# Gate and up by Strassen's scheme in a four-layer residual kernel: seven block products for eight

## The chip, the cores and the metric

The kernel runs on one core of one Trainium2 chip. The metric is the device time of one execution in microseconds (us); lower is better. Three executions of the kernel before took 313.84, 312.49 and 316.62 us, median 313.84.

## The reference, cut to what matters

`x` is 8 batches of 128 tokens with 512 features, all float32. Four layers follow one another, and each adds its result to `x`. Layers 0 to 2 (a weight matrix chosen by each batch's id; a routed low-rank layer; a low-rank layer with a bias) stay as they are. The change is in layer 3, a gated MLP of 1376 hidden features, padded to 11 chunks of 128, with rank-16 additions chosen by batch:

```
def lora_add(base, inp, A, B):
    Ab = A[layer_idx][lora_indices]
    Bb = B[layer_idx][lora_indices]
    t = jnp.einsum('bri,bni->bnr', Ab, inp)
    return base + jnp.einsum('bor,bnr->bno', Bb, t) * SCALE
gate = lora_add(jnp.einsum('bnh,fh->bnf', x, W_gate), x, A_gate, B_gate)
up = lora_add(jnp.einsum('bnh,fh->bnf', x, W_up), x, A_up, B_up)
act = jax.nn.silu(gate) * up
down = lora_add(jnp.einsum('bnf,hf->bnh', act, W_down), act, A_down, B_down)
```

## The kernel before

Everything lies with features on the 128 partitions and the 1024 tokens (two halves `h` of 512) along the free dimension. PE (TensorE) multiplies in fp32r. To keep float32 accuracy each operand is split into a high part, the fp32r copy made by ACT (`high`, line 436), and a low part, the difference made by DVE (`low`, line 619). One product of weights 128x128 with 512 tokens is then three matmuls, lines 967 to 969 (`split_product`).

Gate and up of one chunk `fc` take, for each half and for each of gate and up (`g`), four feature blocks by three matmuls, 12 in all (`gate_up_main`), and then two matmuls of 256 columns that add the ranks (`gate_up_lora`, line 1076, on `bgu_st` and `t3_st`). The sum gathers in one PSUM bank (banks 4 to 7). When the gate bank is done ACT takes its silu into `act_f` (line 558); when the up bank is done DVE multiplies (`act_product`, line 829). Each engine has its own in-order program and they meet at semaphores. Ten of the eleven chunks run in loops of two chunks on every engine. While PE works on a chunk, ACT and DVE split the next chunk's weights (`gate_up_hi`, `gate_up_lo`), and SP loads the chunk after that: one transfer `wgu` and eight transfers `bgu`, one for each batch (`load_gate_up`, lines 357 and 360).

Ahead of the loops stands the entry to layer 3: `thin3` (1052) and `sum_ranks` (1063) make the ranks of `x`, which ACT and DVE write to `t3_st` (436 and 820), and PE does chunk 0 between them. After the loops come the ranks of the down layer (`down_ranks`, line 1123, 176 small matmuls), and then the down product, 22 pieces of at least 12 matmuls, whose activations ACT and DVE split into a ring of eight buffers. In this kernel `wd` is split during the last two chunks of gate and up.

## Time and profile before

| what | us |
|---|---|
| median of three executions | 313.84 |
| the profiled execution | 312.77 |
| its span, first to last instruction | 310.8 |
| PE busy | 302.0 (97%) |
| DVE busy | 146.8 (47%) |
| ACT busy | 106.8 (34%) |

The span leaves about 2 us of the profiled execution's time outside. The busy share of an engine is an average over stages. A PE row's duration overlaps the next one's: the step from one row's start to the next one's is what a matmul costs, and it is read from the timeline.

### The profile page before, as it was taken

How to read it: one execution, taken by the hardware profiler on the slowest of the kernel's cores; microseconds unless marked ns; L12 is line 12 of the kernel's file. 1: busy time of each engine (PE TensorE's matmuls, PEld its weight loads, DVE VectorE, ACT ScalarE, POOL GpSimd, SP SyncE). 2: the span in 40 equal slices, each digit the busy share in tenths (PEclk: the TensorE clock that was granted, in tenths of full speed). 3: DMA queues.
4: the chain of work that ended last, by engine and by line, in shares of the span. 5: the costliest groups of instructions: out<-in, count | busy, mean ns of one | idle time of the engine just before them, and what ended most of it. 6: DMA issues, size and time to landing. Idle time of an engine off the chain costs nothing.

```text
span 310.8 us, 4638 instructions
## 1 busy us (share of the span) xinstructions
PE 302.0 (97%) x1690; PEld 249.1 (80%) x1690; DVE 146.8 (47%) x253; ACT 106.8 (34%) x169; POOL 11.2 (4%) x25
## 2 busy tenths in 40 slices
PE   6799999999999999999999999999999999999995
PEld 5357878988888888888888888888888888888884
DVE  1298898977559336144044043142624833233003
ACT  2377762504335245124034033133532641221000
POOL 1020000800100000000000000000000000000000
PEclk9999999999999999999999999999999999999999
DMA  5989990005206500431421421460520000022004
GB/s 170 343 306 350 396 307 24 2 27 183 63 10 179 160 19 1 137 102 33 135 95 40 135 85 50 146 268 0 162 67 0 2 2 0 0 70 68 0 2 135
DMA packets 23888, 33.21 MB, mean 107 GB/s; under 512 B 3264, under 2 KB 16064, under 8 KB 23744
## 3 DMA queue, kind: packets, MB, share of 16 engines
q1 hardware_dynamic: 23584, 32.48, 32.1%
q10 hardware_dynamic: 288, 0.52, 0.6%
q8 instruction: 10, 0.16, 0.2%
q14 instruction: 6, 0.05, 0.0%
HBM read 30.89 MB, written 2.10 MB: 106 GB/s over the span
## 4 chain that ended last, share of the span: by engine, by line
PE 91%; DMA 3%; SPq 2%; DVE 2%; ACT 1%; issue 0%
PE bank L967 25%; PE bank L968 25%; PE bank L969 25%; PE bank L1076 3%; DMA w_raw<-in_w 3%; PE bank L921 3%; PE bank L1123 2%; PE bank L951 1%; PE bank L1014 1%; PE bank L901 1%; PE bank L953 1%; PE bank L952 1%; PE bank L943 1%; SPq L310 1%; PE bank L1052 1%; PE bank L1023 1%
## 5 line engine op out<-in xcount | busy, mean ns | idle before, releaser
L967 PE MATMUL bank<-xb,wgu_hl 128*128 128x512 f32 x176 | 69.3, 394 | 0.0
L968 PE MATMUL bank<-xb,wgu_hl 128*128 128x512 f32 x176 | 69.0, 392 | 0.0
L969 PE MATMUL bank<-xb,wgu_hl 128*128 128x512 f32 x176 | 68.5, 389 | 0.0
L829 DVE TENSOR_TENSOR act_f<-bank,act_f 128x512 f32 (+1 forms) x22 | 15.2, 692 | 79.4 <-PE bank L1076 75.0
L969 PEld LDWEIGHTS bank<-xb,wgu_hl 128*128 128x128 f32 x176 | 33.1, 188 | 7.2
L967 PEld LDWEIGHTS bank<-xb,wgu_hl 128*128 128x128 f32 x176 | 33.0, 188 | 5.9 <-issue 0.2
L968 PEld LDWEIGHTS bank<-xb,wgu_hl 128*128 128x128 f32 x176 | 33.2, 189 | 5.2
L967 PE MATMUL bank<-act_hl,wd_hl 128*128 128x512 f32 (+1 forms) x99 | 36.5, 369 | 0.0
L968 PE MATMUL bank<-act_hl,wd_hl 128*128 128x512 f32 (+1 forms) x99 | 36.3, 367 | 0.0
L969 PE MATMUL bank<-act_hl,wd_hl 128*128 128x512 f32 (+1 forms) x99 | 36.2, 366 | 0.0
L558 ACT ACTIVATE act_f<-bank 128x512 f32 (+1 forms) x22 | 13.2, 598 | 64.6 <-PE bank L1076 64.6
L619 DVE TENSOR_TENSOR w_hl<-w_raw,w_hl 128x512 fp32r<-128x512 f32 x29 | 19.2, 693 | 9.7 <-ACT w_hl L436 9.7
L619 DVE TENSOR_TENSOR act_hl<-act_f,act_hl 128x512 fp32r<-128x512 f32 x22 | 14.4, 689 | 18.9 <-ACT act_hl L436 18.8
L436 ACT ACTIVATE w_hl<-w_raw 128x512 fp32r<-128x512 f32 x29 | 17.7, 625 | 12.4 <-DMA w_raw<-in_w 12.3
L436 ACT ACTIVATE act_hl<-act_f 128x512 fp32r<-128x512 f32 x22 | 12.9, 626 | 25.3 <-PE bank L969 22.0
L969 PEld LDWEIGHTS bank<-act_hl,wd_hl 128*128 128x128 f32 x99 | 18.6, 188 | 3.1
L967 PEld LDWEIGHTS bank<-act_hl,wd_hl 128*128 128x128 f32 x99 | 18.7, 189 | 3.0 <-issue 0.2
L968 PEld LDWEIGHTS bank<-act_hl,wd_hl 128*128 128x128 f32 x99 | 18.7, 189 | 2.7
L1076 PEld LDWEIGHTS bank<-t_st,bgu_st 128*128 128x128 f32 x88 | 16.1, 188 | 3.5 <-DVE t_st L820 0.2
L436 ACT ACTIVATE wgu_hl<-wgu_raw 128x1024 fp32r<-128x1024 f32 x11 | 11.7, 1061 | 18.4 <-PE bank L1076 18.4
L1076 PE MATMUL bank<-t_st,bgu_st 128*128 128x256 f32 x88 | 17.2, 282 | 0.0
L436 ACT ACTIVATE xb<-x_f 128x512 fp32r<-128x512 f32 x16 | 10.0, 628 | 16.9 <-DVE x_f L739 12.8
(124 smaller groups left out, 418.0 us busy)
## 6 DMA issues: line engine op xcount, KB each, us to landing
w_raw<-in_w SPq DMA_DIRECT2D x22, 256.0 KB, 8.0
wgu_raw<-in_wgu SPq DMA_DIRECT2D x11, 512.0 KB, 3.4
bgu_raw<-in_bgu SPq DMA_DIRECT2D x88, 64.0 KB, 2.2
w_raw<-in_w SPq DMA_DIRECT2D x7, 512.0 KB, 7.8
wd_raw<-in_wd SPq DMA_DIRECT2D x4, 704.0 KB, 5.3
out<-x_f SPq DMA_DIRECT2D x7, 256.0 KB, 2.3
...
```

Source lines behind the costliest of these rows:

```text
L310: _, ids = nc.values_load_multi_w_load_instructions(src[0:1, 0:B], engines=[mybir.EngineType.SP], min_val=0, max_val=last, skip_runtime_bo ...
L436: return act.activation(dst, src, ACT.Copy)
L558: act.activation(act_f[:, fc, h * HT:(h + 1) * HT], bank[4 + 2 * h][:], ACT.Silu).then_inc(silu_done, 1)
L619: return dve.tensor_tensor(dst, src, hi.bitcast(F32), ALU.subtract)
L829: dve.tensor_tensor(dst, bank[5 + 2 * h][:], dst, ALU.mult).then_inc(act_mul, 1)
L901: ins = pe.transpose(dst[:, k * P:(k + 1) * P], src, ident[:])
L921: ins = pe.matmul(thin1_bank(h, j)[:, 0:2 * TM1], xb[:, k, c, cols], aw1_hl[:, c].rearrange("p k n -> p (k n)"), start=(c == 0 and k == 0) ...
L967: pe.matmul(dst, w_hi, x[0][:, cols], start=start, stop=False)
L968: pe.matmul(dst, w_hi, x[1][:, cols], start=False, stop=False)
L969: return pe.matmul(dst, w_lo, x[0][:, cols], start=False, stop=stop)
L1076: ins = pe.matmul(bank[4 + 2 * h + g][:, q * 2 * S:(q + 1) * 2 * S], bgu_st[slot][:, pair, g], t3_st[:, g, pair * 2 * S:(pair + 1) * 2 * S ...
L1123: ins = pe.matmul(bank[h][32 * j:32 * j + R, 0:S], ad_raw[:, b, fc], act_f[:, fc, b * S:(b + 1) * S], start=(fc == 0), stop=(fc == FC - 1))
```

## The change

Chunk 0 stays. The other ten chunks are taken in five pairs, and for each pair gate and up apart, so ten steps `n` (even: gate, odd: up). In one step the 256 output features, 512 input features and 1024 tokens are cut in two each way. The eight block products become seven, in Winograd's form of Strassen's scheme: DVE forms four sums of weight blocks in each step (`form_s`, 128x256 each) and, once, four sums of blocks of `x` (`form_t`, 128x1024 each), all of which are split into high and low as well. Products share banks: ACT copies four partial results of each step from PSUM to SBUF (`copy_part`), and DVE adds them to the finished banks (`add_c`). Silu and the multiplication then read SBUF. Each step has the same eight rank matmuls per two chunks that it had before.

The rank weights of two chunks come in one transfer per batch (`load_bgu`), into one buffer. The loops are written out. The splitting of `wd` moves behind gate and up, piece by piece with the activations. The selection matrices are loaded and spread somewhat later.

The core of the diff:

```diff
...
+            def load_wgu(fc):
+                sp.dma_start(wgu_raw[raw_slot(fc)][:], wgu[fc]).then_inc(wgu_in[raw_slot(fc)], 16)
+            def load_bgu(p):
+                f1, f2 = chunks_of(2 * p)
                 for b in range(B):
                     rows = slice(64 * (b % 2), 64 * (b % 2) + 64)
-                    sp.dma_start(bgu_raw[slot][rows, b // 2], bgu[adapter3[b], fc]).then_inc(bgu_in[slot], 16)
+                    sp.dma_start(bgu_raw[rows, :, b // 2],
+                                 bgu[adapter3[b], f1:f2 + 1].rearrange("f r n -> r f n")).then_inc(bgu_in, 16)
...
-            with sp.Fori(0, 4) as i:
-                for u in range(2):
-                    fc = 2 * i + 2 + u
-                    sp.wait_ge(wgu_lo, 2 * i + 1 + u)
-                    sp.wait_ge(bgu_ready, 2 * i + 1 + u)
-                    load_gate_up(fc, u)
-            sp.wait_ge(wgu_lo, FC - 2)
-            sp.wait_ge(bgu_ready, FC - 2)
-            load_gate_up(FC - 1, 0)
-            sp.wait_ge(bgu_ready, FC)
+            sp.wait_ge(wgu_lo, 1)
+            sp.wait_ge(bgu_ready, 1)
+            sp.wait_ge(main_done, 16)
+            load_bgu(0)
+            load_wgu(3)
+            load_wgu(4)
+            for p in range(1, PAIRS):
+                sp.wait_ge(bgu_ready, bgu_count(2 * p - 1, 1))
+                load_bgu(p)
+                if p + 1 < PAIRS:
+                    sp.wait_ge(wc_lo, 3 * 2 * p)
+                    load_wgu(2 * p + 3)
+                    load_wgu(2 * p + 4)
+            sp.wait_ge(bgu_ready, bgu_count(2 * PAIRS - 1, 1))
+            sp.wait_ge(wc_lo, 3 * 2 * PAIRS)
+            for o in range(C):
+                sp.dma_start(wd_raw[:, o], wd[o]).then_inc(wd_in[o], 16)
...
+            def copy_part(n, k):
+                done, b = ((p1_done, 0), (p5_done, 2), (p6_done, 0), (p7_done, 0))[k]
+                act.wait_ge(done, n + 1)
+                if n == 0:
+                    act.wait_ge(xt_lo, 2)
+                if n >= 2:
+                    act.wait_ge(silu_done if n % 2 == 0 else act_mul, H + 4 * (n // 2))
+                high(part[n % 2][k][:], bank[4 * (n % 2) + b][:]).then_inc(part_copied, 1)
+            def silu(p, k):
+                i, h = c_place(k)
+                fc = chunks_of(2 * p)[i]
+                act.wait_ge(c_added, 8 * p + k + 1)
+                act.activation(act_f[:, fc, h * HT:(h + 1) * HT], part[0][C_PART[k]][:], ACT.Silu).then_inc(silu_done, 1)
...
+                if g == 1:
+                    for k in (2, 3):
+                        silu(p, k)
+                if more:
+                    wc_high(n + 1, 0)
+                copy_part(n, 0)
+                copy_part(n, 1)
+                if more:
+                    wc_high(n + 1, 1)
+                copy_part(n, 2)
+                if more:
+                    wc_high(n + 1, 2)
+                if g == 0:
+                    for k in (0, 1):
+                        silu(p, k)
+                copy_part(n, 3)
+                if more:
+                    for i in range(2):
+                        bgu_high(n + 1, i)
...
+            act.wait_ge(c22_ready, 2 * PAIRS)
+            for i in range(5):
+                wd_high(i)
+                if i == 0:
+                    act.wait_ge(act_mul, 2 * FC)
                 act_high(i)
...
+            def form_s(n, k):
...
+                    ins = dve.tensor_tensor(s_tmp[:, 0], a["21"], a["22"], ALU.add)
+                elif k == 1:
+                    dve.wait_ge(s_formed, 4 * n + 1)
+                    ins = dve.tensor_tensor(s_tmp[:, 1], s_tmp[:, 0], a["11"], ALU.subtract)
+                elif k == 2:
+                    ins = dve.tensor_tensor(s_tmp[:, 2], a["11"], a["21"], ALU.subtract)
+                else:
+                    dve.wait_ge(s_formed, 4 * n + 3)
+                    ins = dve.tensor_tensor(s_tmp[:, 3], a["12"], s_tmp[:, 1], ALU.subtract)
+                ins.then_inc(s_formed, 1)
...
+            def form_t(k):
+                b11, b12, b21, b22 = (x_f[:, h * HB:(h + 1) * HB, 2 * d:2 * d + 2] for d in range(2) for h in range(H))
+                if k == 0:
+                    dve.wait_ge(x_sum, number(2, 1, 1) + 1)
+                    ins = dve.tensor_tensor(tx[0][:], b12, b11, ALU.subtract)
+                elif k == 1:
+                    dve.wait_ge(x_sum, number(2, 1, 3) + 1)
+                    dve.wait_ge(xt_formed, 1)
+                    ins = dve.tensor_tensor(tx[1][:], b22, tx[0][:], ALU.subtract)
+                elif k == 2:
+                    ins = dve.tensor_tensor(tx[2][:], b22, b12, ALU.subtract)
+                else:
+                    dve.wait_ge(xt_formed, 2)
+                    ins = dve.tensor_tensor(tx[3][:], b21, tx[1][:], ALU.subtract)
+                ins.then_inc(xt_formed, 1)
...
             residual(2, 0, [])
             t2_uv_low(1)
-            gate_up_lo(0, 0, 1)
+            odd_lo()
             t2_low(1)
-            gate_up_lo(1, 1, 2)
-            residual(2, 1, [])
+            for k in (0, 2, 1, 3):
+                form_s(0, k)
+            for part_of in range(3):
+                wc_low(0, part_of)
+            x_add(2, 1, 0)
+            x_add(2, 1, 1)
+            x_low(2, 1, 0)
+            form_t(0)
+            x_low(2, 1, 1)
+            x_add(2, 1, 2)
+            x_low(2, 1, 2)
+            x_add(2, 1, 3)
+            form_t(1)
+            x_low(2, 1, 3)
+            for k in range(2, 4):
+                form_t(k)
...
+            def add_c(n, k):
+                ready, b = ((c11_ready, 1), (c12_ready, 2), (c21_ready, 3), (c22_ready, 0))[k]
+                dve.wait_ge(ready, n + 1)
+                dve.wait_ge(part_copied, 4 * n + C_PART[k] + 1)
+                dst = part[n % 2][C_PART[k]]
+                dve.tensor_tensor(dst[:], bank[4 * (n % 2) + b][:], dst[:], ALU.add).then_inc(c_added, 1)
+            def act_product(p, k):
+                i, h = c_place(k)
+                dst = act_f[:, chunks_of(2 * p)[i], h * HT:(h + 1) * HT]
+                dve.wait_ge(silu_done, H + 4 * p + k + 1)
+                dve.wait_ge(c_added, 8 * p + 4 + k + 1)
+                dve.tensor_tensor(dst, part[1][C_PART[k]][:], dst, ALU.mult).then_inc(act_mul, 1)
...
-            act_product(0, 0)
+            for k in range(3):
+                xt_low(k)
+            odd_product(0)
+            for k in (0, 2, 1, 3):
+                form_s(1, k)
             t3_low(1)
+            odd_product(1)
+            for i in range(2):
+                bgu_low(0, i)
+            xt_low(3)
+            for n in range(2 * PAIRS):
+                p, g = divmod(n, 2)
+                more = n + 1 < 2 * PAIRS
+                if more and n > 0:
+                    form_s(n + 1, 0)
+                    form_s(n + 1, 2)
+                if n > 0:
+                    for k in (2, 3):
+                        add_c(n - 1, k)
+                if more:
+                    if n > 0:
+                        form_s(n + 1, 1)
+                    wc_low(n + 1, 0)
+                    if n > 0:
+                        form_s(n + 1, 3)
+                if n > 0 and g == 0:
+                    for k in (2, 3):
+                        act_product(p - 1, k)
+                add_c(n, 0)
+                if g == 1:
+                    act_product(p, 0)
+                if more:
+                    for part_of in (1, 2):
+                        wc_low(n + 1, part_of)
+                add_c(n, 1)
+                if g == 1:
+                    act_product(p, 1)
+                if more:
+                    for i in range(2):
+                        bgu_low(n + 1, i)
             for h in range(H):
                 zero_td_bank(h)
...
+            for k in (2, 3):
+                add_c(2 * PAIRS - 1, k)
+                act_product(PAIRS - 1, k)
...
+            def product(dst, n, a, x, start, stop):
+                w = wc[1 - n % 2]
+                for c in range(2):
+                    hi, lo = w[:, 0, a, c], w[:, 1, a, c]
+                    pe.matmul(dst[:], hi, x[0][c], start=(start and c == 0), stop=False, skip_group_check=True)
+                    pe.matmul(dst[:], hi, x[1][c], start=False, stop=False, skip_group_check=True)
+                    ins = pe.matmul(dst[:], lo, x[0][c], start=False, stop=(stop and c == 1), skip_group_check=True)
+                return ins
+            def step3(n):
+                p, g = divmod(n, 2)
+                f1, f2 = chunks_of(n)
+                x, w, y, z = (bank[4 * g + k] for k in range(4))
+                pe.wait_ge(wc_lo, 3 * n + 1)
+                if n >= 2:
+                    pe.wait_ge(c_added, 4 * (n - 1))
+                product(x, n, A11, x_block(0, 0), True, True).then_inc(p1_done, 1)
+                product(w, n, A12, x_block(1, 0), True, False)
+                pe.wait_ge(bgu_ready, bgu_count(n, 0))
+                lora3(w, f1, g, 0).then_inc(c11_ready, 1)
+                pe.wait_ge(wc_lo, 3 * n + 2)
+                if n == 0:
+                    pe.wait_ge(xt_lo, 1)
+                product(y, n, S1, t_block(0), True, True).then_inc(p5_done, 1)
+                pe.wait_ge(part_copied, 4 * n + 1)
+                if n == 0:
+                    pe.wait_ge(xt_lo, 2)
+                product(x, n, S2, t_block(1), False, True).then_inc(p6_done, 1)
+                pe.wait_ge(part_copied, 4 * n + 2)
+                product(y, n, S4, x_block(1, 1), False, False)
+                lora3(y, f1, g, 1).then_inc(c12_ready, 1)
+                pe.wait_ge(part_copied, 4 * n + 3)
+                if n == 0:
+                    pe.wait_ge(xt_lo, 3)
+                product(x, n, S3, t_block(2), False, True).then_inc(p7_done, 1)
+                pe.wait_ge(wc_lo, 3 * n + 3)
+                if n == 0:
+                    pe.wait_ge(xt_lo, 4)
+                product(z, n, A22, x_block(0, 1), True, False)
+                pe.wait_ge(bgu_ready, bgu_count(n, 1))
+                lora3(z, f2, g, 0).then_inc(c21_ready, 1)
+                pe.wait_ge(part_copied, 4 * n + 4)
+                lora3(x, f2, g, 1).then_inc(c22_ready, 1)
...
```

The places that the prediction speaks of, in each engine's own order. First ACT, one odd step before: here the loop over one chunk, between two silu.

```order
L436 ACTIVATE wgu_hl_89<-wgu_raw_85 128x1024 [waits up_done]
L436 ACTIVATE bgu_st_87<-bgu_raw_83 128x1024 [waits bgu_in1]
L557 ISA
L558 ISA [waits gate_done]
L558 ACTIVATE act_f<-bank 128x512
```

And ACT now, in the whole of step 3 (odd; `wc_gate` holds the weights of step 4, `part_0` and `part_1` are the partial results of gate and of up, whose last digits number buffers).

```order
L664 ACTIVATE act_f<-part_3_101 128x512 [waits c_added]
L664 ACTIVATE act_f<-part_1_99 128x512 [waits c_added]
L498 ACTIVATE wc_gate<-wgu_raw_88 128x512 [waits wgu_in3,wgu_in2,c21_ready]
L498 ACTIVATE part_0_102<-bank 128x512 [waits act_mul,p1_done]
L498 ACTIVATE part_1_103<-bank 128x512 [waits act_mul,p5_done]
L498 ACTIVATE wc_gate<-s_tmp 128x1024 [waits s_formed]
L498 ACTIVATE part_2_104<-bank 128x512 [waits act_mul,p6_done]
L498 ACTIVATE wc_gate<-wgu_raw_89 128x256
L498 ACTIVATE part_3_105<-bank 128x512 [waits act_mul,p7_done]
L498 ACTIVATE bgu_st_84<-bgu_raw 128x4x128 [waits c22_ready,bgu_in]
L498 ACTIVATE bgu_st_83<-bgu_raw 128x4x128 [waits c22_ready,bgu_in]
```

Two silu and a weight split now stand ahead of the first copy of a partial result.

DVE ahead of them, from the end of step 2 into step 3.

```order
L924 SCALAR_TENSOR_TENSOR bgu_st_84<-bgu_st_84,lo_rows_128,bgu_raw 128x4x128 [waits bgu_hi]
L924 SCALAR_TENSOR_TENSOR bgu_st_83<-bgu_st_83,lo_rows_128,bgu_raw 128x4x128 [waits bgu_hi]
L946 TENSOR_TENSOR s_tmp<-wgu_raw_89 128x256 [waits wc_lo,wgu_in3,wgu_in2]
L951 TENSOR_TENSOR s_tmp<-wgu_raw_88,wgu_raw_89 128x256
L1038 TENSOR_TENSOR part_3_101<-bank,part_3_101 128x512 [waits part_copied,c21_ready]
L1038 TENSOR_TENSOR part_1_99<-bank,part_1_99 128x512 [waits part_copied,c22_ready]
```

The two sums that the silu need stand behind two splits of rank weights and two weight sums. Before, nothing of this was on DVE.

DVE at the entry to layer 3, between the end of `t2` and the first rank write `t_st` (before: two `x_f` at once, no `tx`).

```order
L869 SCALAR_TENSOR_TENSOR x_f<-bank,bias_sb,x_f 128x4x128 [waits main_done]
L749 TENSOR_TENSOR xb<-x_f,xb 128x512 [waits x_hi]
L869 SCALAR_TENSOR_TENSOR x_f<-bank,bias_sb,x_f 128x4x128 [waits main_done]
L976 TENSOR_TENSOR tx_94<-x_f,tx_93 128x1024 [waits xt_formed,x_sum]
L749 TENSOR_TENSOR xb<-x_f,xb 128x512 [waits x_hi]
L978 TENSOR_TENSOR tx_95<-x_f 128x1024
L981 TENSOR_TENSOR tx_96<-x_f,tx_94 128x1024 [waits xt_formed]
L1022 SCALAR_TENSOR_TENSOR t_st<-t_st,hi_lo,bank 64x2x128 [waits t3_hi,hi_lo_copied]
```

The three `tx` rows (`form_t`) now stand ahead of the rank write.

## Rows read from the trace of the kernel before

**Rows 1.** The page: busy us, share of the span, instructions.
```profile
PE 302.0 (97%) x1690; PEld 249.1 (80%) x1690; DVE 146.8 (47%) x253; ACT 106.8 (34%) x169; POOL 11.2 (4%) x25
```
**Rows 2.** The page: chain that ended last, share of the span by engine.
```profile
PE 91%; DMA 3%; SPq 2%; DVE 2%; ACT 1%; issue 0%
```
**Rows 3.** Stretches: us, busy PE, PEld, DVE, ACT, POOL; granted clock, DMA share, GB/s.
```profile
0.00:42.60 42.60, 37.29 (x164) 26.16 (x165) 27.47 (x51) 25.05 (x45) 3.11 (x9) 1.00 0.91 318
...
103.40:119.60 16.20, 16.20 (x138) 13.47 (x138) 6.88 (x14) 6.17 (x14) 0.00 (x0) 1.00 0.23 70
119.60:238.80 119.20, 119.20 (x565) 99.44 (x567) 41.75 (x42) 35.33 (x43) 0.00 (x0) 1.00 0.29 95
```
**Rows 4.** Timeline in one chunk: start us, us, engine, line, operation, [idle before].
```profile
179.05 0.40 PE L967 MATMUL bank<-xb,wgu_hl 128*128 128x512 f32 x1
...
181.80 0.40 PE L1076 MATMUL bank<-t_st,bgu_st 128*128 128x256 f32 x2
182.03 0.40 PE L967 MATMUL bank<-xb,wgu_hl 128*128 128x512 f32 x1
...
182.32 0.60 ACT L558 ACTIVATE act_f<-bank 128x512 f32 x1 [1.06 <-PE bank L1076]
...
183.60 5.05 SPq L360 DMA_DIRECT2D bgu_raw<-in_bgu  x8
...
185.01 0.40 PE L967 MATMUL bank<-xb,wgu_hl 128*128 128x512 f32 x1
...
185.39 0.69 DVE L829 TENSOR_TENSOR act_f<-bank,act_f 128x512 f32 x1 [2.62 <-PE bank L1076]
```
**Rows 5.** Groups by line and form: count, busy us, mean ns, idle before.
```profile
L619 DVE TENSOR_TENSOR act_hl<-act_f,act_hl 128x512 fp32r<-128x512 f32 x22 | 14.4, 689 | 18.9 <-ACT act_hl L436 18.8
L797 DVE SCALAR_TENSOR_TENSOR bgu_st<-bgu_st,lo_rows,bgu_raw 128x1024 fp32r<-128x1024 f32 x11 | 14.1, 1278 | 0.0
L619 DVE TENSOR_TENSOR wgu_hl<-wgu_raw,wgu_hl 128x1024 fp32r<-128x1024 f32 x11 | 13.5, 1225 | 2.4 <-ACT wgu_hl L436 2.4
L436 ACT ACTIVATE act_hl<-act_f 128x512 fp32r<-128x512 f32 x22 | 12.9, 626 | 25.3 <-PE bank L969 22.0 <-DVE act_f L829 3.2
L436 ACT ACTIVATE wgu_hl<-wgu_raw 128x1024 fp32r<-128x1024 f32 x11 | 11.7, 1061 | 18.4 <-PE bank L1076 18.4
L829 DVE TENSOR_TENSOR act_f<-bank,act_f 128x512 f32 x16 | 11.1, 692 | 62.9 <-PE bank L1076 62.9
L558 ACT ACTIVATE act_f<-bank 128x512 f32 x16 | 9.6, 600 | 51.1 <-PE bank L1076 51.1
```
**Rows 6.** Timeline, ACT and DVE: six instructions in a row without a gap.
```profile
239.71 3.23 ACT L436 ACTIVATE act_hl<-act_f 128x512 fp32r<-128x512 f32 x6 [3.24 <-DVE act_f L829]
240.37 3.70 DVE L619 TENSOR_TENSOR act_hl<-act_f,act_hl 128x512 fp32r<-128x512 f32 x6 [0.76 <-ACT act_hl L436]
```
**Rows 7.** The page: DMA issues, count, KB each, us from issue to landing.
```profile
bgu_raw<-in_bgu SPq DMA_DIRECT2D x88, 64.0 KB, 2.2
...
wd_raw<-in_wd SPq DMA_DIRECT2D x4, 704.0 KB, 5.3
```
**Rows 8.** Timeline of DVE and of PE at the entry to layer 3.
```profile
96.03 1.23 DVE L619 TENSOR_TENSOR wgu_hl<-wgu_raw,wgu_hl 128x1024 fp32r<-128x1024 f32 x1
98.37 1.40 DVE L739 SCALAR_TENSOR_TENSOR x_f<-bank,bias_sb,x_f 128x512 f32<-128x512 f32 x2
108.84 2.02 DVE L820 SCALAR_TENSOR_TENSOR t_st<-t_st,hi_lo,bank 64x256 fp32r<-64x256 f32 x4 [3.18 <-ACT t_st L436]
116.80 2.01 DVE L820 SCALAR_TENSOR_TENSOR t_st<-t_st,hi_lo,bank 64x256 fp32r<-64x256 f32 x4 [1.76 <-ACT t_st L436]
...
112.00 0.74 PE L1076 MATMUL bank<-t_st,bgu_st 128*128 128x256 f32 x4
118.93 0.69 PE L1076 MATMUL bank<-t_st,bgu_st 128*128 128x256 f32 x4
```
**Rows 9.** The chain in order of time: start us, us, what (the down ranks).
```profile
238.82 4.93 PE bank L1123 x176
```

349 lines of the change are left out of this document (210 added, 139 removed).

## The prediction, made before the changed kernel had run

> **What bounds the kernel now.** I read the busy shares first: PE is busy for 302.0 of 310.8 us, DVE for 47% and ACT for 34% [rows 1]. Then the chain: PE holds 91% of it [rows 2]. Then the stretches: in the loops over chunks 1 to 10, 119.60 to 238.80, PE is busy without a gap and its granted clock is 1.00, that is 2.4 GHz, while DVE works 41.75 and ACT 35.33 of 119.20 us [rows 3]. So removed PE work is worth its full time there, as long as DVE and ACT stay ahead. Last the timeline of one chunk, for prices. The twelve matmuls of 512 columns run from 179.05 to 181.80, 0.229 us each, and the two rank matmuls from 181.80 to 182.03, 0.23 us [rows 4]; a group repeats every 2.98 us (182.03 to 185.01). The 0.40 beside each row overlaps its neighbours and is no price.
>
> **PE.** Before, two chunks of gate (or up) took 2 x 2 x 12 = 48 matmuls of 512 columns and 8 of 256. A step now takes 7 products x 2 feature blocks x 3 = 42, and the same 8. Ten steps save 60 matmuls x 0.229 = **13.7 us**. A step lasts 42 x 0.229 + 4 x 0.23 = 10.55 us where it was 4 x 2.98 = 11.92. The form (128x128 weights, 512 columns) doesn't change. Within a step, counted from its start, P1 ends at 1.37, c11 is ready at 2.98, P5 ends at 4.35 and P6 at 5.72, c12 is ready at 7.3, P7 ends at 8.7, c21 is ready at 10.3, c22 at 10.55.
>
> **DVE and ACT in a step.** DVE takes 689 ns for 512 elements and 1225 for 1024 [rows 5], so about 1.05 ns an element, and by that line 0.42 us for 256. In a queue without waits six of 512 take 3.70 us, so 0.60 from one to the next, 0.09 less than one alone; on ACT six take 3.23, so 0.52, 0.10 less [rows 6]. The rank split (1278 for 1024 [rows 5]) gives 0.74 for 512. A DVE step: four weight sums 4 x 0.42, four `add_c` 4 x 0.69, three weight splits 0.69 + 1.23 + 0.42, two products 2 x 0.69, two rank splits 2 x 0.74 = 9.7 us alone, 8.4 when queued (15 instructions, 0.09 less each). That is 80 to 92% of 10.55, where it was 35% [rows 3]. ACT: splits 0.63 + 1.06 + 0.41, four copies and two silu at 0.60 [rows 5], two rank copies at 0.63 = 7.0 alone, 5.9 queued. Neither is the bound by its sum; what matters is the round trip through both.
>
> **The round trip.** PE to ACT takes 0.29 us (the group ends at 182.03, silu starts at 182.32), PE to DVE 0.38 (185.01 to 185.39) [rows 4]. P7 ends at 8.7, so its copy starts at 9.0 and the two rank copies at 9.5 and 10.0; DVE splits them at 10.2 and 10.8 and is free at 11.5, that is 0.9 into the next step. There come two weight sums (0.9, 1.25), then `add_c` for c21 and c22 (1.6 and 2.2, done at 2.9). In an **odd** step ACT's queue has silu of these two first: at 2.35 and 3.0, then the weight split at 3.5, then the copy of P1 at 4.0, done at 4.6. PE needs it at 4.35, to add P6 to the same bank. With 0.1 us to take the signal up, PE waits about 0.4 us. In an **even** step ACT has no silu there, and P1's copy starts at 1.7; later `silu(p, 1)` needs `add_c` of c12, at 7.75 to 8.45 on DVE, so P7's copy starts at 9.1 and is done at 9.7, where PE needs it at 10.3: no wait. The last odd step has no weight split, and no wait. So 4 x 0.4 = **+1.6 us**, between 0 (hand-overs 0.1 shorter at four places) and 4.8 (twelve instructions of the round trip each 0.07 longer).
>
> Here DVE reads PSUM in `add_c`. The product that reads a bank takes 692 ns, the split from SBUF 689 [rows 5], so the sum takes one price for both. The Trainium skill (VectorE: DVE Perf Modes, "The TRN2 errata") gives a PSUM source 62 cycles more on VectorE, 0.065 us; by it the two `add_c` on the round trip would add 0.13 us in each of four odd steps, +0.5. The two rows, equal but for 3 ns, don't show that.
>
> **The entry.** DVE starts a weight split at 96.03 and reaches `x_add` of the second half at 98.37 [rows 8]. Now four weight sums and three splits stand there, with ACT's splits between: sums to 97.6 (four steps, one link dependent), the second split can start when ACT's 1.06 us copy is done, at 98.8, and the last ends at 100.3. `x_add` comes 1.9 us later; PE took up that half's work well after it. But `form_t` adds four of 1.23 us, and DVE reaches the first rank write at about 110.9, done (2.02 us) at 112.9, where it was 108.84 to 110.86; PE wants the ranks at 112.00 [rows 8], so it waits 0.9. Behind it stand three splits of `xt` (3.4 queued), a product, four sums (1.6): the second rank write starts at 118.7 and ends at 120.7, where PE, 0.9 late, wants it at 119.8: another 0.9. Together **+1.8 us**; bounds 0.5 (if the queue spacing holds at each place) and 4 (if each of some twenty instructions takes 0.1 longer).
>
> **The end.** `wd` is no longer split beforehand. It is loaded after the last rank split, 1 us into step 9. One transfer of 704 KB of the four took 5.3 us in the median [rows 7]; four at once I take as at most 9.5, which ends at the end of the step. The last two `add_c` and products end 2.7 us after the step; then ACT 0.63 and DVE 0.69: the first piece is ready 4.3 us after it, and PE's down ranks cover 4.93 [rows 9]. Afterwards a piece costs DVE 1.2 and PE some 2.7. I take **+0.2**, bounds 0 and 2.5 (a load later by two). The later selection matrices and the POOL work lie on no chain: +0. One transfer per batch halves the issues (eight took 5.05 us on SP [rows 4]), which ran beside PE and are worth nothing.
>
> **Sum.** -13.7 + 1.6 + 1.8 + 0.2 = -10.1 us. Against the profiled execution (312.77) that gives 302.7; the median of the three stands 1.07 higher and gives 303.7. I take **303.2**.
>
> **Rivals.**
> - *The round trip is wider.* For it: DVE at up to 92%, and 25 instructions a step that wait for another engine. Against it: queued spacing is 0.09 shorter than durations. If each of twelve links costs 0.1 more, odd steps lose 1.2 more (x4) and even steps, with 0.6 of slack in P7's copy, 0.3 (x5): +6.3, about **309.5**. Chance 0.15.
> - *No wait at all.* The walk was pessimistic, or PE's own starts drift late enough to cover it: 313.3 - 13.7 = **299.6**. Chance 0.10.
> - *The one rank buffer makes it slower.* The new load starts only after the second rank split of the odd step, 1.2 us into it, its last issue goes out at 6.3 and lands at 8.5 if it takes the 2.2 us of the row [rows 7] though it is twice as large. ACT wants it at 9.5; PE itself only 3.0 us into the next step, at 13.5, so a landing after about 12.2 delays PE, in four steps. From 14.7 on (8.4 us from issue to landing) the 10.1 us are gone, and at 16.4 it is **320**. Against it: DMA is at 0.29 in that stretch [rows 3]. Chance 0.03.
> - *The clock falls.* PE now waits for ACT inside a step. Before, PE was idle for 5.3 of the first 42.6 us and the clock stayed at 1.00 [rows 3], so short waits did not lower it here. One step at 1.2 GHz would cost 10.5 us more: **313.7**. Chance 0.04. The Trainium skill (TensorE: Matmul & The Clock Gate, "A second HAM failure mode: psum-queue depth-cycling") tells of a kernel that cycled through PSUM banks, idled briefly between groups and had its clock switch back and forth; the loops here cycled through four banks at 1.00, which speaks against it.
>
> **How the numbers follow.** My forecast has 0.68, with 300.5 to 307 as its own spread from the bounds. The range 299.5 to 308.5 takes in that, half of the case without waits and a third of the wider round trip: about 0.78. Two per cent, which is about what can be told from no change here (the three executions differ by 1.3%), is 6.3 us: faster means below 307.6. Forecast, no wait and a fifth of the wider round trip: 0.81. Within 2%: the rest of it and the clock, 0.16. Slower: 0.03.
>
> **What the profile after would show.** PE with 60 matmuls fewer and steps of 10.55 us (even) and 10.9 (odd), 0.229 from start to start. A PE gap before the first matmul that adds P6 in odd steps, put down to ACT's copy, none in even steps. DVE at 8 to 9.7 busy us a step. PE gaps of about 0.9 before the two rank groups at the entry, put down to DVE's `t_st`. No gap after the down ranks. I'm wrong if even steps show gaps, if ACT waits for `bgu_raw`, if a wait at the end stands on `wd`, or if the clock is below 1.00.

## The result, and the profile of the changed kernel

The changed kernel takes **302.89 us** (median of four executions, 302.5 to 303.19) where the kernel before takes 313.74 (312.49 to 316.62): a ratio of 0.9642, with a 95% interval of 0.9605 to 0.9679. The forecast was 303.2. The profiled execution took 302.71 us, of which the span is 300.9; before, these were 312.77 and 310.8.

The page first: busy time, share of the span and instructions of each engine, and then the chain of work by engine.

```profile
PE 290.3 (96%) x1630; PEld 237.4 (79%) x1630; DVE 204.4 (68%) x378; ACT 142.4 (47%) x250; POOL 10.7 (4%) x25
PE 64%; DVE 13%; SPq 7%; DMA 6%; issue 4%; ACT 4%; DVEq 0%; ACTq 0%
```

60 matmuls are gone from PE. Against [rows 1] DVE has 57.6 us more work and ACT 35.6. PE's part of the chain falls from 91% [rows 2] to 64%, which looks like a new bound but isn't one: PE is still busy for 96% of the span. The chain now crosses places where PE waited for a few tenths, and from there it follows the engine that released it far back. Only the stretches tell how much such a place costs.

The stretches of both kernels, cut at the same events: the first rank matmul of layer 3, the first matmul of step 0, the first matmul of the down ranks. Columns as in [rows 3]. Before:

```profile
103.41:119.45 16.04, 16.04 (x137) 13.31 (x137) 6.88 (x14) 6.02 (x14) 0.00 (x0) 1.00 0.23 71
119.45:238.82 119.37, 119.37 (x566) 99.61 (x568) 41.75 (x42) 35.48 (x43) 0.00 (x0) 1.00 0.29 95
```

After, with one even step (step 0), one odd step (step 1) and the down ranks behind them:

```profile
103.74:121.38 17.64, 16.61 (x137) 13.24 (x137) 15.99 (x24) 9.39 (x18) 0.96 (x1) 1.00 0.37 120
121.38:228.74 107.36, 106.94 (x503) 88.06 (x501) 81.11 (x140) 62.58 (x109) 0.00 (x0) 1.00 0.28 96
121.38:132.00 10.62, 10.62 (x53) 8.86 (x52) 7.09 (x10) 8.65 (x15) 0.00 (x0) 1.00 0.00 0
132.00:142.81 10.81, 10.81 (x52) 8.74 (x51) 8.23 (x16) 6.00 (x11) 0.00 (x0) 1.00 0.51 161
228.74:233.66 4.92, 4.92 (x177) 4.71 (x176) 4.61 (x8) 2.76 (x6) 0.00 (x0) 1.00 0.46 132
```

The span is 9.9 us shorter. Ten steps give 119.37 - 107.36 = 12.01. The entry takes 1.60 of it back (16.04 to 17.64), and layer 3 starts 0.33 later (103.41 to 103.74), ahead of everything that the diff puts behind it. From the first down-rank matmul to the end it is 71.9 before and 72.2 after, 0.2 more; of this the down ranks are 4.85 and 4.92 (up to 243.67 and 233.66, the first matmuls of the down product). The granted clock is 1.00 in every stretch. DVE works 8.1 us in a step of 10.7, ACT 6.3.

The ten steps last 10.62, 10.81, 10.61, 10.82, 10.60, **11.25**, 10.61, 10.81, 10.61 and 10.62 us. So four odd steps are longer, and one of them more than the others.

The entry, on PE: the three rows before which PE waited, in the same view as [rows 8].

```profile
107.94 1.16 PE L1308 MATMUL bank<-t_sb,t_sel 128*128 128x128 f32 x8 [0.17 <-ACT t_sb L498]
...
113.26 0.71 PE L1321 MATMUL bank<-t_st,bgu_st 128*128 128x256 f32 x4 [0.40 <-DVE t_st L1022]
...
120.81 0.74 PE L1321 MATMUL bank<-t_st,bgu_st 128*128 128x256 f32 x4 [0.46 <-DVE t_st L1022]
```

And DVE there:

```profile
100.46 1.40 DVE L869 SCALAR_TENSOR_TENSOR x_f<-bank,bias_sb,x_f 128x512 f32<-128x512 f32 x2
...
111.10 2.01 DVE L1022 SCALAR_TENSOR_TENSOR t_st<-t_st,hi_lo,bank 64x256 fp32r<-64x256 f32 x4
...
118.74 2.01 DVE L1022 SCALAR_TENSOR_TENSOR t_st<-t_st,hi_lo,bank 64x256 fp32r<-64x256 f32 x4
```

The two rank writes start at 111.10 and 118.74, and PE takes each up 0.15 and 0.06 us after its end. DVE is late by its queue, without idle time in front of either row.

The round trip of step 5, the long one, which starts at 174.84. DVE's sum is done, ACT runs two silu, then a weight split, then the copy of P1, and PE takes up P6:

```profile
177.49 1.23 ACT L664 ACTIVATE act_f<-part 128x512 f32<-128x512 f32 x2 [2.23 <-DVE part L1038]
...
179.77 0.50 PE L1342 MATMUL bank<-xt,wc_up 128*128 128x512 f32 x1 [0.42 <-ACT part L498]
```

In steps 1, 3 and 7 the same place shows no bracket, and has to be read from the starts. This is step 1, which starts at 132.00:

```profile
134.21 1.23 ACT L664 ACTIVATE act_f<-part 128x512 f32<-128x512 f32 x2 [2.23 <-DVE part L1038]
135.35 0.61 ACT L498 ACTIVATE wc_gate<-wgu_raw 128x512 fp32r<-128x512 f32 x1
135.87 1.28 ACT L498 ACTIVATE part<-bank 128x512 f32<-128x512 f32 x2
...
136.13 0.39 PE L1344 MATMUL bank<-xt,wc_up 128*128 128x512 f32 x1
136.50 0.50 PE L1342 MATMUL bank<-xt,wc_up 128*128 128x512 f32 x1
136.84 0.39 PE L1343 MATMUL bank<-xt,wc_up 128*128 128x512 f32 x1
```

From start to start these take 0.37 and 0.34 us where the neighbours take 0.23: 0.25 more in all. The first is the matmul that adds P6 into P1's bank, and the copy ahead of it began at 135.87.

Two readings were not forecast. The load of rank weights, on SP's queue and on ACT, which waits for it in steps 1 and 3 (they start at 132.00 and 153.42):

```profile
133.08 6.14 SPq L413 DMA_DIRECT2D bgu_raw<-in_bgu  x8
...
142.11 1.15 ACT L498 ACTIVATE bgu_st<-bgu_raw 128x512 fp32r<-128x512 f32 x2 [0.33 <-DMA bgu_raw<-in_bgu]
...
154.50 6.08 SPq L413 DMA_DIRECT2D bgu_raw<-in_bgu  x8
...
163.96 1.15 ACT L498 ACTIVATE bgu_st<-bgu_raw 128x512 fp32r<-128x512 f32 x2 [0.76 <-DMA bgu_raw<-in_bgu]
```

Eight issues take 6.1 us, 0.77 each, where eight of half the size took 5.05 [rows 4]. They land 3.5 and 4.0 us after the last of them started (138.62 and 159.97, see the last section), and so 10.1 and 10.5 us into the step. The page has 2.7 for the median where it had 2.2 [rows 7]:

```profile
bgu_raw<-in_bgu SPq DMA_DIRECT2D x40, 128.0 KB, 2.7
```

Last the end. ACT splits the first piece of the activations 2.8 us after the steps' end, and DVE's part of it is done at 232.88, 0.78 ahead of PE, which leaves the down ranks at 233.66:

```profile
231.53 0.63 ACT L498 ACTIVATE act_hl<-act_f 128x512 fp32r<-128x512 f32 x1 [2.06 <-DVE act_f L1045]
...
232.19 0.69 DVE L749 TENSOR_TENSOR act_hl<-act_f,act_hl 128x512 fp32r<-128x512 f32 x1
```

### The profile page after: what moved, and what is told of

Its sections match the earlier page's. It is cut to its first block, busy times and chain, and to the rows that moved or that the text cites. A ratio compares the mean times of both kernels' runs of the same rounds, so it can differ in the third digit from the quotient of the medians.

```text
span 300.9 us, 4565 instructions
## 1 busy us (share of the span) xinstructions
PE 290.3 (96%) x1630; PEld 237.4 (79%) x1630; DVE 204.4 (68%) x378; ACT 142.4 (47%) x250; POOL 10.7 (4%) x25
## 4 chain that ended last, share of the span: by engine, by line
PE 64%; DVE 13%; SPq 7%; DMA 6%; issue 4%; ACT 4%; DVEq 0%; ACTq 0%
PE bank L1212 11%; PE bank L1213 11%; PE bank L1214 11%; PE bank L1342 6%; PE bank L1343 6%; PE bank L1344 6%; DMA w_raw<-in_w 4%; SPq L413 3%; SPq L358 3%; DMA bgu_raw<-in_bgu 2%; PE bank L1321 2%; PE bank L1166 2%; DVE bgu_st L924 2%; DVE part L1038 2%; PE bank L1416 2%
## 5 line engine op out<-in xcount | busy, mean ns | idle before, releaser
L498 ACT ACTIVATE part<-bank 128x512 f32<-128x512 f32 x40 | 23.7, 595 | 26.8 <-PE bank L1344 26.2
L1038 DVE TENSOR_TENSOR part<-bank,part 128x512 f32<-128x512 f32 x40 | 26.7, 685 | 5.1 <-PE bank L1321 3.8
L924 DVE SCALAR_TENSOR_TENSOR bgu_st<-bgu_st,lo_rows,bgu_raw 128x512 fp32r<-128x512 f32 (+1 forms) x21 | 15.4, 773 | 14.3 <-ACT bgu_st L498 14.3
L498 ACT ACTIVATE act_hl<-act_f 128x512 fp32r<-128x512 f32 x22 | 13.6, 624 | 20.8 <-PE bank L1214 18.8
L664 ACT ACTIVATE act_f<-part 128x512 f32<-128x512 f32 x20 | 12.5, 632 | 15.7 <-DVE part L1038 15.7
L1072 DVE TENSOR_TENSOR x_f<-bank,x_f 128x512 f32<-128x512 f32 (+1 forms) x9 | 5.5, 629 | 19.5 <-PE bank L1437 19.5
L1321 PEld LDWEIGHTS bank<-t_st,bgu_st 128*128 128x128 f32 x88 | 14.7, 188 | 3.9 <-DVE t_st L1022 0.9
L1321 PE MATMUL bank<-t_st,bgu_st 128*128 128x256 f32 x88 | 15.8, 284 | 0.9 <-DVE t_st L1022 0.9
L1344 PE MATMUL bank<-xb,wc_gate 128*128 128x512 f32 x40 | 15.7, 394 | 0.0
L1343 PE MATMUL bank<-xb,wc_gate 128*128 128x512 f32 x40 | 15.7, 392 | 0.0
L1342 PE MATMUL bank<-xb,wc_up 128*128 128x512 f32 x40 | 15.6, 391 | 0.0
L1343 PE MATMUL bank<-xb,wc_up 128*128 128x512 f32 x40 | 15.6, 390 | 0.0
```

What stands on the lines that cost most here:

```text
L498: return act.activation(dst, src, ACT.Copy)
L664: act.activation(act_f[:, fc, h * HT:(h + 1) * HT], part[0][C_PART[k]][:], ACT.Silu).then_inc(silu_done, 1)
L924: return dve.scalar_tensor_tensor(out=st, in0=st.bitcast(F32), scalar=lo_rows16[:, 0:1], in1=raw, op0=ALU.mult, op1=ALU.add)
L1038: dve.tensor_tensor(dst[:], bank[4 * (n % 2) + b][:], dst[:], ALU.add).then_inc(c_added, 1)
L1321: ins = pe.matmul(dst[:, q * 2 * S:(q + 1) * 2 * S], bgu_st[fc % 2][:, pair, g], t3_st[:, g, pair * 2 * S:(pair + 1) * 2 * S], start=False ...
L1342: pe.matmul(dst[:], hi, x[0][c], start=(start and c == 0), stop=False, skip_group_check=True)
```

## Experiments

**Theory.** PE's work is the gain. It is short by a wait for P1's copy in four odd steps, set by the length of the round trip (DVE's sums, ACT's silu, ACT's split, ACT's copy) and not by how much DVE or ACT do in a step. **Rivals:** DVE, at 8.1 us a step, is near its bound, so that any work added to it costs time; the combining frame of the scheme costs PE something of its own; and the merged load of rank weights, which I had called worthless, carries part of the result. Step lengths are given throughout, since the profiled executions reach layer 3 anywhere between 102.9 and 104.7 us, while the ten steps of the two kernels that were profiled twice agree within 0.2%. Each kernel was timed beside the kernel before on the same chip (313.46, 313.59, 313.25 and 313.17 us in the four groups).

### The changed kernel again, and the two waits taken away one by one

The first group has the changed kernel itself, as it stands.

> The changed kernel once more, unedited, so that the three edits of this group are compared with it on the same chip. 302.9 us, 10.9 below the kernel before; odd steps of 10.8 us, the third of them (step 5) up to 0.4 longer, even steps of 10.6 us.

Measured: 303.25 us, ratio 0.9689 (0.9663 to 0.9714). Entry 17.65, steps 107.56 together, step 5 again the longest (11.39).

Then P1's copy, ahead of the silu in odd steps:

```diff
                 if g == 1:
+                    copy_part(n, 0)
                     for k in (2, 3):
                         silu(p, k)
                 if more:
                     wc_high(n + 1, 0)
-                copy_part(n, 0)
+                if g == 0:
+                    copy_part(n, 0)
                 copy_part(n, 1)
```

> Edit: in odd steps ACT copies the first partial result (P1) ahead of the two silu and the weight split, not behind them. Theory (the round trip through DVE and ACT makes PE wait for that copy in odd steps): the wait goes and every step takes 10.62 us; the trace of the changed kernel has the four odd steps 0.20, 0.20, 0.63 and 0.20 us above that, so 1.2 us less than the unedited kernel, 301.7. Rival (the extra length of odd steps is bank switching or a weight load, not the copy): no change, 302.9, with the gap still ahead of the first S2 matmul.

Measured: 301.64 us, ratio 0.9640 (0.9613 to 0.9667); entry 17.65, steps 105.76 together: 10.61, **10.53**, 10.60, **10.54**, 10.60, **10.53**, 10.60, **10.53**, 10.60, 10.62. ACT in step 1, which starts at 132.13 here:

```profile
133.71 0.60 ACT L498 ACTIVATE part<-bank 128x512 f32<-128x512 f32 x1 [1.60 <-PE bank L1346]
134.35 1.23 ACT L664 ACTIVATE act_f<-part 128x512 f32<-128x512 f32 x2
```

The copy is done at 134.31, and PE gets to P6 some 4.35 us into the step, at 136.5, and the wait is gone in all four steps. An odd step without it takes 10.53, less than an even one. So the round trip costs 0.28 us in steps 1, 3 and 7, which is about what the starts above show, and 0.72 in step 5: 1.56 together, and that is all that steps 0 to 9 lose to waits.

Next the entry: `form_t(3)` behind the first rank write, the second rank write ahead of the product and the weight sums, and ACT's split of `xt` out of the way.

```diff
-            for k in range(2, 4):
-                form_t(k)
+            form_t(2)
...
             t3_low(0)
+            form_t(3)
             for k in range(3):
                 xt_low(k)
+            t3_low(1)
             odd_product(0)
             for k in (0, 2, 1, 3):
                 form_s(1, k)
-            t3_low(1)
             odd_product(1)
```

> Edit: at the entry to layer 3 the rank writes t_st come earlier in DVE's and ACT's queues: the fourth sum of x blocks behind the first rank write, the first product of chunk 0 and the weight sums of step 1 behind the second, and on ACT the copy of the second sum of x blocks behind the first rank copy. Theory (PE waits there for DVE's queue alone): the gaps of 0.40 and 0.46 us before the two groups of rank matmuls go, with the slower restart after each, and step 0 begins 1.1 us earlier: 301.8. Rival (what is moved comes back as a wait in steps 0 and 1, where xt, the rank split and the product of chunk 0 are then late): 302.9, with new gaps in step 0.

Measured: 301.31 us, ratio 0.9628 (0.9605 to 0.9650). The entry takes 16.50 and step 0 10.82, 0.21 more than before the edit, since its first rank matmul now waits for DVE's split of `bgu_st`. Step 5 takes 10.80: its extra 0.44 is gone, although nothing in it was edited. In this execution ACT waited for the load of rank weights by 0.08 us in step 1 and not at all in step 3, where it had waited 0.76; the experiments on the load, below, return to this.

> Both edits, of ACT's order in odd steps and of the entry. If the two waits are separate, the gains add: 2.3 us less than the unedited kernel, 300.6. If one hides the other, 301.7.

Measured: 301.06 us, ratio 0.9611 (0.9587 to 0.9636). By stage both gains are there (entry 16.52, steps 105.97: 2.5 us less than the changed kernel; step 5's extra 0.44, which either edit alone also lost, counts once). The median is only 0.25 us under that of the entry edit alone and lies between the two forecasts; the profiled execution reached layer 3 at 104.65, about 1 us later than the others. In a second group, below, the median is 300.65.

### Is the removed work worth its full time?

The eighth product comes back, in the place where a step has its last one. The kernel counts A22 twice in c21; everything else of the scheme stays.

```diff
                 product(z, n, A22, x_block(0, 1), True, False)
+                product(z, n, A22, x_block(0, 1), False, False)
                 pe.wait_ge(bgu_ready, bgu_count(n, 1))
```

> Edit: an eighth product in each of the ten steps: the product of A22 is made twice into its bank, behind P7 (its rows of gate and up come out too large by it). It gives back the 60 matmuls. Theory (the gain is removed PE work and nothing else, and the odd steps' wait is a round trip from P7 to the next step, which now has 1.36 us more): 60 x 0.227 = +13.6 us, less the 1.2 us of waits, +12.4: 315.3, so 1 to 2 us slower than the kernel before, with all steps at 12.0. Rival (sharing banks and writing the loops out are worth something by themselves): 313.7 or less. Rival (the waits stay): 316.5.

Measured: 315.66 us, ratio 1.0068 (1.0041 to 1.0095), without a PE wait in a step.

```profile
121.16:240.55 119.39, 119.39 (x563) 99.59 (x561) 81.74 (x140) 62.27 (x109) 0.00 (x0) 1.00 0.26 86
```

With 48 matmuls of 512 columns a step the ten steps take 119.39 us, and 119.37 in the kernel before. So 40 us of new DVE work and 27 of new ACT work (41.75 to 81.74, 35.48 to 62.27) cost PE nothing while it ran, and what the scheme costs outside PE's count is the 2.07 us by which this kernel is slower: the entry (17.64, 1.6 more) and 0.5 elsewhere. Against the 105.76 of the kernel with P1's copy first, 60 matmuls make 13.6 us, 0.227 each. With a longer step the wait in odd steps vanished too, as a round trip from P7 asks: the eighth product stands behind P7, so ACT and DVE have 1.4 us more until the next step.

### The trip, or the load on DVE?

One instruction of 0.68 us more on DVE in each of four odd steps (it sums `x_f` into a scratch tile). In the first kernel, whose edit is shown, it stands on the trip, ahead of the sums of c21 and c22; in the second it stands later in the same step, ahead of the first rank split, where DVE was idle.

```diff
+        scratch = own("scratch", [2 * PAIRS, C])
...
                     form_s(n + 1, 2)
+                if more and g == 1:
+                    dve.tensor_reduce(scratch[:, n], x_f[:, 0], AX_X, ALU.add)
```

> Edit: one more DVE instruction (a sum over 512 elements of x into a scratch tile, about 0.6 us) in steps 1, 3, 5 and 7, between the weight sums and the two add_c, that is on the round trip from P7 to the copy of P1. Theory (the wait is the round trip): each of the four steps grows by about 0.6 us, +2.4: 305.3, and the wait before the first S2 matmul is 0.8. Rival (DVE's sum counts, not its place): same as the other placing of it.

> Edit: the same DVE instruction in the same four steps, but ahead of the first rank split, where DVE waits 1 to 1.9 us for ACT. Theory: +0, 302.9, though DVE is as busy as with the other placing. Rival (DVE's sum counts): +2.4, 305.3.

Measured: on the trip 305.37 us, ratio 0.9744 (0.9714 to 0.9774); in the gap 303.12, ratio 0.9666 (0.9642 to 0.9691). Steps 110.02 and 107.68 together. DVE and PE in step 1 of the kernel with it on the trip (one more line stands above, so 1038 is 1039 here):

```profile
133.59 0.68 DVE L1094 TENSOR_REDUCE scratch<-x_f 128x4 f32<-128x512 f32 x1
134.18 1.28 DVE L1039 TENSOR_TENSOR part<-bank,part 128x512 f32<-128x512 f32 x2
...
137.18 0.50 PE L1345 MATMUL bank<-xt,wc_up 128*128 128x512 f32 x1 [0.55 <-ACT part L499]
```

The same instruction costs 2.34 us in the one place and nothing in the other. PE waits 0.55 before P6; by the starts, P6's second matmul comes 0.83 later than in a step without a wait, where 0.8 was forecast. DVE has slack; the path has none. The even steps of both kernels are 0.16 us longer, which is not the instruction's doing; see the last section.

### The load of rank weights

The load as it was, one transfer per batch and chunk, but into the one raw buffer (ACT waits for each half by its own semaphore):

```diff
-                f1, f2 = chunks_of(2 * p)
-                for b in range(B):
-                    rows = slice(64 * (b % 2), 64 * (b % 2) + 64)
-                    sp.dma_start(bgu_raw[rows, :, b // 2],
-                                 bgu[adapter3[b], f1:f2 + 1].rearrange("f r n -> r f n")).then_inc(bgu_in, 16)
+                for i, fc in enumerate(chunks_of(2 * p)):
+                    for b in range(B):
+                        rows = slice(64 * (b % 2), 64 * (b % 2) + 64)
+                        sp.dma_start(bgu_raw[rows, i, b // 2],
+                                     bgu[adapter3[b], fc]).then_inc((bgu_in, bgu_in2)[i], 16)
```

> Edit: the rank weights of a pair come in two transfers per batch again, 16 issues in place of 8, all else as in the changed kernel. My prediction held the merging to be worth nothing. Theory now, by the trace of the changed kernel (8 issues took 6.1 us, landing came 3.5 to 4.0 us after the last, 10.1 to 10.5 us into the odd step, and ACT already waited up to 0.8 us for it): 16 issues at 0.63 take 10 us and land 14 us after the start of the odd step, 3.4 us into the even one; ACT's queue is then blocked ahead of the copy of P1, and PE waits 1 to 2 us in each of four even steps and somewhat in the odd step behind: +4 to +9 us, 307 to 312. Rival (hidden anyway): 302.9.

Measured: 313.05 us, ratio 0.9977 (0.9956 to 0.9998), 1 us above the forecast range. The steps take 116.80 us together, 9.4 more. In steps 1 and 2, which start at 132.07 and 142.90:

```profile
133.16 10.93 SPq L413 DMA_DIRECT2D bgu_raw<-in_bgu  x16
...
145.70 0.63 ACT L498 ACTIVATE bgu_st<-bgu_raw 128x512 fp32r<-128x512 f32 x1 [3.31 <-DMA bgu_raw<-in_bgu]
...
146.76 1.32 ACT L498 ACTIVATE part<-bank 128x512 f32<-128x512 f32 x2
...
150.29 1.06 ACT L498 ACTIVATE wc_up<-s_tmp 128x1024 fp32r<-128x1024 f32 x1 [2.21 <-DVE s_tmp L954]
151.25 0.58 ACT L498 ACTIVATE part<-bank 128x512 f32<-128x512 f32 x1
...
151.88 0.50 PE L1342 MATMUL bank<-xt,wc_gate 128*128 128x512 f32 x1 [1.24 <-ACT part L498]
```

Sixteen issues hold SP for 10.93 us, and the load lands 13.6 us after the start of step 1. ACT stands in its queue in front of the load, 3.31 us, and with it stand the weight splits and the copies of step 2 that are queued behind. The copy of P1, where the wait was forecast, is only 0.12 late for PE in step 2. The large wait stands 9 us into step 2, at the copy of P6: DVE's rank split is late by ACT's, its weight sums stand behind it, ACT's split of these sums waits for them (2.21), and P6's copy stands behind that split. Nowhere does PE wait for the rank weights themselves. So with one raw buffer nearly all of the kernel's gain hangs on the halved count of issues. Sixteen issues with a raw buffer for each chunk, as the kernel before had them, were not run in the changed kernel; whether they would have stayed hidden is open.

Then the other end: no load at all after the first pair. Every step uses the first pair's rank weights.

```diff
-                load_bgu(p)
...
-                act.wait_ge(bgu_in, 16 * B * (n // 2 + 2))
+                act.wait_ge(bgu_in, 16 * B * 2)
```

> Edit: the rank weights are loaded for the first pair only and used for all five (the ranks of the other four pairs come out wrong by it); nothing waits for those transfers. Theory (the extra 0.4 us of step 5 began as ACT's wait for bgu_raw in step 3): ACT has no wait on bgu_raw, all four odd steps are 10.8, total -0.4: 302.5. Rival (step 5's extra wait has another origin): step 5 still 11.25.

Measured: 302.12 us, ratio 0.9644 (0.9606 to 0.9682). Steps 10.58, 10.83, 10.60, 10.81, 10.61, **10.82**, 10.60, 10.81, 10.61, 10.62. The 0.28 in the odd steps stays, and step 5 is one of four equals. The place that waited 0.42 in the changed kernel:

```profile
178.78 0.50 PE L1341 MATMUL bank<-xt,wc_up 128*128 128x512 f32 x1
```

So the 0.44 that step 5 loses beyond the others comes from the load. The other kernels say the same by degrees. ACT's wait for the load is followed two steps later by a longer odd step: 0.76 by 0.44 in the changed kernel, 0.92 by 0.57 and 0.39 by 0.06 when it ran again. Waits of 0.33 (the changed kernel, step 1) and 0.24 (the added instruction in the gap, step 3) are followed by nothing. By these five, some 0.33 us of the wait is free and the rest is passed on one for one. The way from the load to step 5, by rows of the changed kernel, is this: ACT's wait of 0.76 in step 3 puts the rank splits late, so that DVE sums c12 of step 4 late, and silu waits for it, and P7's copy and the next rank split stand behind that silu.

```profile
173.09 0.63 ACT L664 ACTIVATE act_f<-part 128x512 f32<-128x512 f32 x1 [1.43 <-DVE part L1038]
```

That silu starts 8.85 us into step 4 and its fellow in step 2 starts 8.42 into it, 0.43 earlier; in step 5 silu of c21 starts 2.65 us in, and in step 1 2.21. The lag is handed on nearly unchanged for a step and a half. Its two ends are shown (taken away, it's gone); the links between are read from these rows.

### A copy behind the load

The rank splits now stand ahead of P7's copy on ACT, so that the wait for the load would hold the copy up.

```diff
-                copy_part(n, 3)
                 if more:
                     for i in range(2):
                         bgu_high(n + 1, i)
+                copy_part(n, 3)
```

> Edit: on ACT the two copies of the next step's rank weights stand ahead of the copy of P7's partial result, not behind it. It undoes one piece of the order by PE's needs. Theory: in odd steps ACT waits for bgu_raw, which lands 10.1 to 10.5 us into the step, so the copy of P7 starts at 11.3 and ends at 11.9, where PE wants it at 10.4: +1.5 us in four odd steps; in even steps the rank copies (1.1 us) start at 8.9 and the copy ends at 10.6, +0.2 in four: +6 to +7 us, 309 to 310. Rival (the order doesn't matter while ACT is busy for 60%): 302.9.

Measured: 304.35 us, ratio 0.9687 (0.9643 to 0.9730): a miss. The steps are 10.89, **12.01**, 10.89, 10.95, 10.89, **10.54**, 10.90, 10.63, 10.89 and 10.61, together 109.2 us, 1.8 more than in the changed kernel. The forecast wait appears in step 1 and then fades.

```profile
143.09 1.15 ACT L498 ACTIVATE bgu_st<-bgu_raw 128x512 fp32r<-128x512 f32 x2 [3.10 <-DMA bgu_raw<-in_bgu]
144.14 0.58 ACT L498 ACTIVATE part<-bank 128x512 f32<-128x512 f32 x1
144.77 0.50 PE L1321 MATMUL bank<-t_st,bgu_st 128*128 128x256 f32 x2 [1.22 <-ACT part L498]
...
155.04 0.57 ACT L498 ACTIVATE part<-bank 128x512 f32<-128x512 f32 x1
155.22 0.94 PE L1321 MATMUL bank<-t_st,bgu_st 128*128 128x256 f32 x4
...
156.23 6.08 SPq L413 DMA_DIRECT2D bgu_raw<-in_bgu  x8
```

In odd steps PE waits 1.22 in step 1, 0.16 in step 3, and not at all in the next ones. I had kept the load where it was, 1.08 us into an odd step. But the load waits for the second rank split on DVE, and that follows ACT's, which this edit puts earlier: the load now starts 0.22 us into each odd step (133.33 and 156.23 in steps that start at 133.11 and 156.01), 0.86 earlier. In step 1 it still landed 10.0 us into the step, in steps 3, 5 and 7 8.9, 8.5 and 8.6, nearly or wholly early enough for P7's copy. The earlier rank splits shorten the round trip as well: in step 5 silu starts 1.36 us in, not 2.65, and the step has its length without a wait. Most of what the steps lose lies in the even ones, where PE shows no bracket: the last four rank matmuls, of which two need P7's copy, take 0.94 where they took 0.65, 0.29 in each of five steps, 1.4 together (forecast: 0.2 in four). Priced with everything else held fixed, the whole came out over three times too high: 6 to 7 us, where the steps grew by 1.8 and the median by 1.5.

### The version that the experiments point to

Both edits, and on DVE `odd_product(1)` and the first two rank splits ahead of the weight sums of step 1, for the 0.21 us of step 0.

> Edit, on top of both edits (ACT's order in odd steps, the entry): on DVE the weight sums of step 1 stand behind the first rank split, so that the rank weights of step 0 are ready in time. Theory (in the kernel with both edits step 0 is 0.21 us longer than the other even steps because its first rank matmul waits for that split, 124.03 against 123.93): step 0 takes 10.6 us, 0.2 less in all, 300.8. Rival: the weight sums are then late for ACT's split in step 0, and the gap moves to step 1.

> The kernel with both edits once more, unedited, for comparison on the same chip: 301.0 us. Its time and that of the one beside it should differ by less than single executions of one kernel do (1.7 us here), so the difference is read from the stages of the trace.

Measured: 300.32 us for it, ratio **0.9585** (0.9558 to 0.9611), and 300.65 for the two edits alone, ratio 0.9608 (0.9583 to 0.9633).

```profile
102.94:119.45 16.51, 16.34 (x137) 13.24 (x137) 14.55 (x20) 9.61 (x18) 0.95 (x1) 1.00 0.42 129
119.45:225.20 105.75, 105.75 (x502) 88.36 (x500) 82.53 (x145) 62.63 (x109) 0.00 (x0) 1.00 0.30 98
```

The steps are down to 105.75 us without a wait, 0.21 under the two edits alone (105.96), and the entry to 16.51. The difference between the two versions is visible by stage; in the medians it is inside the intervals. Against the kernel before it is 4.1% shorter. The loss by P1's copy is gone, and the entry's is cut from 1.6 to 0.5, nearly all of it a wait for `t_sb` that no edit touched.

## Why the prediction was right, and where it was right by luck

| term | predicted | measured | shown by |
|---|---|---|---|
| PE: 60 matmuls fewer | -13.7 | -13.6 | steps without waits, 105.76 against 119.37; with eight products, 119.39 |
| wait for P1's copy, four odd steps | +1.6 | +1.56 | copy ahead of silu: steps 107.36 to 105.76 |
| entry | +1.8 | +1.60 | stretch 16.04 to 17.64 |
| end | +0.2 | +0.2 | 71.9 to 72.2 from the first down rank on; no cause shown |
| merged transfers | 0 | -9.4 against two per batch into the one buffer | load as it was: 116.80 for the steps |
| ahead of layer 3 | none | +0.33 | not tested; the profiled executions of this study reach layer 3 between 102.9 and 104.7 |

**PE.** Right in kind and size: 0.227 a matmul against 0.229. The clock stayed at 1.00 and the eighth product puts back what seven leave out.

**The round trip.** The mechanism is right: it stands before the first matmul that adds P6, in odd steps but the last, put down to ACT's copy, and it goes with the order on ACT. Its size agrees only in the sum. Alone the trip costs 0.28 a step, not 0.4, so 1.12; DVE's sums started about where the walk had them, and silu at 2.21 where it had 2.35. The other 0.44 is step 5, where the load of step 3 comes out: a cause the walk didn't have. The rivals of a wider trip and of no wait both fall, and the load on DVE is no bound, as the pair with the added instruction shows.

**The entry.** DVE was followed to 0.2 us at each row: `x_f` forecast at 100.3 and seen at 100.46, the first rank write at 110.9 and 111.10, the second at 118.7 and 118.74. The sum, 1.60 beside 1.8, is right in part by luck. Matmul by matmul against the kernel before, the two rank groups lose 0.47 and 0.69 us (brackets 0.40 and 0.46), where 0.9 and 0.9 stood. PE came to them later than forecast: layer 3 began 0.33 later, and a wait for `t_sb` that the prediction didn't have had already cost 0.44 (bracket 0.17, and the matmul behind it is 0.10 late too). ACT's copy to `t_sb` starts 3.88 us after the first rank matmul of layer 3, behind DVE's last `x_f` and its split; before it started 1.43 after it. The three losses make the 1.60. The move of the rank writes gave 1.15 back; the wait for `t_sb` stands in every version. A gap in brackets understates a wait, since it leaves out what the next matmuls start late.

**The end.** As forecast there is no wait: the first piece of activations was ready 4.1 us after the steps (forecast 4.3) under 4.92 of down ranks. The 0.2 itself is luck. The prediction had no mechanism for it, PE shows no gap there, and the down product takes 63.24 us from its first matmul to its last before and 63.22 after; the rest lies in the down ranks (0.07) and behind the last matmul of the down product, and nothing here tests it.

**The step that failed** is one that left the time right: "One transfer per batch halves the issues (eight took 5.05 us on SP), which ran beside PE and are worth nothing." Before, that was so, with a rank buffer for each chunk. In the changed kernel one buffer for two chunks gives the load a start (DVE's last rank split, 1.08 into an odd step) and an end (ACT's next rank split, 9.8 into it) under 9 us apart, and in that window sixteen issues of 10.93 us don't fit. I had worked out the window in the rival of the one rank buffer, but never put the unmerged load through it. By the rival's own numbers it would have landed at 1.2 + 16 x 0.63 + 2.2 = 13.5 us (an estimate; 13.6 was seen in step 1) and cost 1.3 us in four steps, about 5 us: half of the gain, and no longer nothing. In the kernel with two transfers ACT waited 12.5 us in all, over four odd steps, and PE's steps took 9.4 longer.

That the rival's price is still too low has a reason of its own. It counted from PE's use of the rank weights, so that a landing before 12.2 was free. The rows show that the loss comes through ACT's queue, and begins near 10.1. The landing was off as well: I took 5.1 us for the issues and 2.2 behind them, 8.5 us into the step. In the trace the last issue started 5.5 us after the first, and the load landed 3.5 and 4.0 after that, 10.1 and 10.5 us into the step. "ACT waits for `bgu_raw`" was on my list of what would prove me wrong; ACT did wait, by 0.33 and 0.76, and that cost 0.44 us. That it was no more is luck: by the five waits above a landing later still would have been passed on one for one (an estimate from these waits; none of them is longer than 0.92).

**The rules weighed.** The Trainium skill (VectorE: DVE Perf Modes, "The TRN2 errata") asks 62 cycles more for a PSUM source. The rows of the changed kernel speak against it, both forms side by side in one execution, the sum that reads a bank and the product that reads SBUF alone:

```profile
L1038 DVE TENSOR_TENSOR part<-bank,part 128x512 f32<-128x512 f32 x40 | 26.7, 685 | 5.1 <-PE bank L1321 3.8 <-ACT part L498 1.3
L1045 DVE TENSOR_TENSOR act_f<-part,act_f 128x512 f32<-128x512 f32 x20 | 13.5, 691 | 1.3
```

685 ns with the bank and 691 without: no addition. What the Trainium skill (TensorE: Matmul & The Clock Gate, "A second HAM failure mode: psum-queue depth-cycling") tells of a clock that switches back and forth when PE idles briefly between groups did not show here either. PE waited up to 1.24 us inside steps of the kernel with two transfers, cycling through eight banks, and the granted clock was 1.00 over its ten steps.
